# Folding a row stage (x + bias + two matrix products) into the tiles of a graph layer, with the layer's sum turned round

## The reference, cut to what matters

```python
xn = layernorm(x)
x = x + gnn(xn, edge_index, W1, b1, W2, b2) + mix(xn, W_qkv, b_qkv, W_out, b_out)
x = x + ffn(layernorm(x), ...)
# gnn: z = relu(agg(xn @ W1) + b1); z = relu(agg(z @ W2) + b2), agg over 200000 edges and self loops
# mix: attn = v + q2 @ kv / sqrt(N); return attn @ W_out + b_out
```

## Time and profile before

| | |
|---|---|
| median of 3 runs | 2124.17 us (2123.45 to 2128.42) |
| profiled execution, its own time | 2122.97 us |
| its span, first to last instruction | 2121.1 us |
| TensorE busy | 1900.7 us (90%) |
| VectorE, ScalarE, GpSimd busy | 1179.8, 878.9, 289.1 us |
| granted TensorE clock, mean | 0.951 of full speed |

### The profile page before, as it was taken

How to read it: one execution, slowest core, us unless ns; L and a number is a source line. 1 busy time by engine, 2 the same in 40 slices (tenths; PEclk the granted TensorE clock), 3 DMA queues, 4 the chain that set the end, 5 groups by cost and what they waited for, 6 DMA issues and landing times. The chain is left out here.

```text
span 2121.1 us, 37341 instructions
## 1 busy us (share of the span) xinstructions
PE 1900.7 (90%) x11735; PEld 1126.4 (53%) x11735; DVE 1179.8 (56%) x2764; ACT 878.9 (41%) x1997; POOL 289.1 (14%) x418
## 2 busy tenths in 40 slices
PE   3069997969999999999999799999999999999588
PEld 3045555845555555555555445555555555555477
DVE  6368872255666656566666235555555555555422
ACT  2157770035555555555555323333333333333200
POOL 3502222310000000000000200000000000000033
PEclk7579998989999999999999999999999999999789
DMA  3113325922222222222222344334343434342078
GB/s 92 31 43 112 111 98 180 285 81 107 107 91 121 91 121 91 116 96 102 110 91 121 120 152 141 141 134 148 127 154 123 156 123 156 125 146 102 20 235 249
DMA packets 106576, 262.52 MB, mean 124 GB/s; under 512 B 15682, under 2 KB 73386, under 8 KB 93978
## 3 DMA queue, kind: packets, MB, share of 16 engines
q1 hardware_dynamic: 76245, 225.23, 29.8%
q10 hardware_dynamic: 28116, 32.06, 4.3%
q0 software_dynamic: 2176, 4.75, 0.8%
HBM read 138.39 MB, written 124.42 MB: 124 GB/s over the span
## 5 line engine op out<-in xcount | busy, mean ns | idle before, releaser
L1344 PE MATMUL ps<-hs,at 128*128 128x512 f16 x2401 | 670.5, 378 | 3.3 <-POOL at L1261 3.3
L1539 PE MATMUL ps<-big,at 128*128 128x512 f16 x2401 | 559.7, 380 | 5.9 <-DMA at<-at_scratch 5.9
L1391 ACT CAST at<-ps 128x392 f16<-128x392 f32 x784 | 375.0, 486 | 430.3 <-PE ps L1333 408.4
L1333 PE MATMUL ps<-big 128*128 128x98 f16 x3136 | 465.0, 209 | 11.2 <-DVE big L1289 11.2
L1333 PEld LDWEIGHTS ps<-big 128*128 128x128 f16 x3136 | 298.4, 98 | 151.4 <-issue 10.8
L1539 PEld LDWEIGHTS ps<-big,at 128*128 128x128 f16 x2401 | 233.5, 98 | 255.6 <-issue 10.5
L1344 PEld LDWEIGHTS ps<-hs,at 128*128 128x128 f16 x2401 | 229.9, 97 | 146.3 <-POOL at L1261 3.5
L1289 DVE TENSOR_TENSOR big<-big,key_lo 128x1024 f16<-128x1024 f16 x392 | 268.5, 685 | 0.0
L1289 DVE TENSOR_TENSOR big<-big,key_hi 128x784 f16<-128x784 f16 x392 | 219.6, 560 | 17.5 <-POOL big L1251 7.6
L1751 POOL TENSOR_TENSOR key_lo<-key_lo,big 128x512 f32<-128x512 f32 (+1 forms) x49 | 61.8, 1262 | 708.0 <-ACT big L1713 708.0
L1300 DVE TENSOR_TENSOR big<-ps,big 128x256 f32<-128x256 f32 x49 | 20.8, 425 | 208.4 <-ACT big L1399 208.4
(11 more groups left out here) (275 smaller groups left out, 2218.4 us busy)
## 6 DMA issues: line engine op xcount, KB each, us to landing
at_scratch<-at SPq DMA_DIRECT2D x49, 1568.0 KB, 5.2
at<-at_scratch SPq DMA_DIRECT2D x49, 1568.0 KB, 6.5
xT_scratch<-big SPq DMA_DIRECT2D x98, 128.0 KB, 1.8
big<-xT_scratch SPq DMA_DIRECT2D x49, 256.0 KB, 3.5
wT_scratch<-big ACTq DMA_DIRECT2D x49, 256.0 KB, 2.1
hs<-wT_scratch SPq DMA_DIRECT2D x49, 256.0 KB, 3.4
big<-in_x_dram SPq DMA_DIRECT2D x96, 128.0 KB, 2.5
base_scratch<-big ACTq DMA_DIRECT2D x48, 128.0 KB, 4.1
```

The source lines that it names most:

```text
L1333: te.matmul(ps[:, BANKS[i // UW % len(BANKS)], i % UW * KC:(i % UW + 1) * KC], lhsT=hot_lo[:, s, :].rearrange("p (q k r) -> p q k r", k=P, ...
L1344: mm = te.matmul(ps[:, 2 + b, :], lhsT=at[:, b, k * P:(k + 1) * P], rhs=hs[:, k, :], start=(k == 0), stop=(k == T - 1))
L1391: a.copy(to.rearrange("p k (i j) -> p k i j", j=WIN), ps[:, BANKS[m % len(BANKS)], 0:UW * KC].rearrange("p (i k j) -> p k i j", i=UW, j=WI ...
L1539: mm = te.matmul(ps[:, b, :], lhsT=at[:, b, k * P:(k + 1) * P], rhs=hs2[:, k, :], start=(k == 0), stop=(k == T - 1))
```

## The change

Stage 0 and `base_scratch` go. Layer 2 loads x and the turned rows itself (128 and 256 KB a tile), GpSimd adds `bvo` to x there, TensorE makes the four products at step 3 of the 49 (`mix`), and VectorE adds them in `norm`. `wvo`, `mkv` and `bvo` get buffers of their own.

The layer 2 sum is turned round: `hs2` is now the stationary operand (four blocks of 128x128) and the block of `at` the moving one (128 columns), so each of 49 steps is four matmuls of 128 columns instead of one of 512. High and low halves add up in PSUM and the sum comes out turned already. So the copy of the low half, `gather`, and `turn` go; `multiply` moves from step 12 to 6.

In layer 1 only places move: `bias` from after batch 5 to 6, `multiply` from build step 28 to 36, `relu` from after unit 12 to 13.

```diff
-        stream(0, big_f, lambda t: xT_dram[...], x, [wvo[:, 0, :], wvo[:, 1, :], mkv[:, 0, :], mkv[:, 1, :]], bvo, base_dram)
...
-                        if i == 5 and reached(t, 1):
+                        if i == 6 and reached(t, 1):
                             bias(t - 1, 1 - b)
...
-                        if i == 28 and reached(t, 1):
+                        if i == 36 and reached(t, 1):
                             multiply(t - 1, 1 - b)
...
-                        if m == 12 and reached(t, 1):
+                        if m == 13 and reached(t, 1):
                             relu(t - 1, 1 - b)
...
-                    sp.dma_start(base_in[0:rows(t), b, :], base_dram[...]).then_inc(base_loaded[b], 16)
+                    sp.dma_start(base_in[0:rows(t), b, :], x[...]).then_inc(base_loaded[b], 16)
+                    sp.dma_start(turned_in[:, b]..., xT_dram[...]).then_inc(base_loaded[b], 16)
...
-                            pe.wait_ge(agg_ready, t - 1)
-                    mm = te.matmul(ps[:, b, :], lhsT=at[:, b, k * P:(k + 1) * P], rhs=hs2[:, k, :],
-                                   start=(k == 0), stop=(k == T - 1))
+                            pe.wait_ge(aggT_ready, t - 1)
+                    for h in range(2):
+                        for c in range(CB):
+                            mm = te.matmul(ps[:, b, c * NT:(c + 1) * NT], lhsT=hs2[:, k, h * C + c * P:h * C + (c + 1) * P],
+                                           rhs=at[:, b, k * P:(k + 1) * P], start=(k == 0 and h == 0 and c == 0),
+                                           stop=(k == T - 1 and h == 1), skip_group_check=True)
...
-                def turn(t, b):
...
+                def mix(t, b, u):
+
+                    pe.wait_ge(base_loaded[b], 32 * u + 32)
+                    if reached(t, 1):
+                        pe.wait_ge(x1_ready, t)
+                    for i, w in enumerate((wvo[:, 0, :], wvo[:, 1, :], mkv[:, 0, :], mkv[:, 1, :])):
+                        mm = te.matmul(ps[:, 2, 0:C], lhsT=turned_in[:, b, i, :], rhs=w, start=(i == 0), stop=(i == 2 * CB - 1))
+                    mm.then_inc(mixed, 1)
...
-                            for at_k, do in ((6, turn), (12, multiply), (31, turn_x), (37, logits)):
+                            if k == 3:
+                                mix(t - 1, *shifted_slot(b, u, -1, 2))
+                            for at_k, do in ((6, multiply), (31, turn_x), (37, logits)):
...
-                def gather(t, b):
-                    dve.wait_ge(low_ready, t + 1)
-                    v.tensor_tensor(agg[0:NT, b, :], ps[0:NT, b, 0:C], low[0:NT, b, :], ALU.add).then_inc(agg_ready, 1)
...
-                    dve.wait_ge(base_loaded[b], 16 * u + 16)
+                    dve.wait_ge(mixed, t + 1)
+                    dve.wait_ge(biased, t + 1)
+                    v.tensor_tensor(base_in[0:NT, b, :], ps[0:NT, 2, 0:C], base_in[0:NT, b, :], ALU.add).then_inc(zb_ready, 1)
...
-                    a.copy(low[0:NT, b, :], ps[0:NT, b, C:2 * C]).then_inc(low_ready, 1)
-                    act.wait_ge(agg_turned, t + 1)
-                    a.copy(aggT[:, b].rearrange("p a b -> p (a b)"), ps[:, 2, 0:CB * NT]).then_inc(aggT_ready, 1)
+                    if reached(t, 2):
+                        act.wait_ge(multiplied, t - 1)
+                    a.copy(aggT[:, b].rearrange("p a b -> p (a b)"), ps[:, b, 0:CB * NT]).then_inc(aggT_ready, 1)
...
+                    if within(t, T - 2):
+                        pool.wait_ge(base_loaded[b], 32 * u + 64)
+                        g.tensor_tensor(base_in[:, b, :], base_in[:, b, :], bvo, ALU.add).then_inc(biased, 1)
```

More of the change, by code:

```diff
@@ L85, in gps_layer @@
     at_dram = nc.dram_tensor("at_scratch", (T, P, T * P), F16, kind="Internal").ap()
-    base_dram = nc.dram_tensor("base_scratch", (N, C), F32, kind="Internal").ap()
     xT_dram = nc.dram_tensor("xT_scratch", (T, P, 2 * CB * NT), F32, kind="Internal").ap()
@@ L140, in gps_layer @@
         eps = sb("eps", [P, 1])
+        wvo = sb("wvo", [P, CB, C])[:, :, :]
+        mkv = sb("mkv", [P, CB, C])[:, :, :]
+        bvo = sb("bvo", [P, C])[:, :]
         ps = life.enter_context(nc.psum_tensor("ps", [P, 8, 512], F32))
@@ L157, in gps_layer @@
         bqk = take([P, 2 * C])
-        wvo = take([P, CB, C])
         bvw = take([P, C])
-        bvo = take([P, C])
-        mkv = take([P, CB, C])
         brow = take([3, 2 * C], BF16)
         ones3 = take([3, P], BF16)
-        AT_USED = 2 * CB * C + 2 * C + CB * C + 2 * C + CB * C + C + P // 2
+        AT_USED = 2 * CB * C + 2 * C + C + C + P // 2
         ones = sb("ones", [P, 2])
@@ L1056, in _ @@
                         act.wait_ge(s_out[b], 16 * (len(range(b, T, NB)) + past_in(b)))
-        stream(0, big_f, lambda t: xT_dram[bass.ds(t, 1)].rearrange("t p n -> (t p) n"), x,
-               [wvo[:, 0, :], wvo[:, 1, :], mkv[:, 0, :], mkv[:, 1, :]], bvo, base_dram)
         BATCH = 7
@@ L1481, in gps_layer @@
             take = carve(big_f[:, T * C:])
-            agg = take([P, 2, C])
-            low = take([P, 2, C])
             aggT = take([P, 2, CB, NT])
@@ L1486, in gps_layer @@
             base_in = take([P, 2, C])
+            turned_in = take([P, 2, 2 * CB, NT])
             x1 = take([P, 2, C])
@@ L1504, in gps_layer @@
             x1_out, w_out = [sem(f"x1_out{b}") for b in range(2)], [sem(f"w_out{b}") for b in range(2)]
-            summed, low_ready, agg_ready = sem("l2_summed"), sem("l2_low_ready"), sem("l2_agg_ready")
-            agg_turned, aggT_ready, multiplied = sem("l2_agg_turned"), sem("l2_aggT_ready"), sem("l2_multiplied")
+            summed, aggT_ready, multiplied = sem("l2_summed"), sem("l2_aggT_ready"), sem("l2_multiplied")
             x1_ready, ln_step, xn2_ready = sem("x1_ready"), sem("l2_ln_step"), sem("xn2_ready")
@@ L1512, in gps_layer @@
             acc_ready = sem("acc_ready")
+            biased, mixed = sem("l2_biased"), sem("l2_mixed")
             block = stage.enter_context(nc.Block())
@@ L1525, in tile @@
                         sp.wait_ge(x1_ready, t - 1)
-                    sp.dma_start(base_in[0:rows(t), b, :], base_dram[bass.ds(t * NT, rows(t)), :]).then_inc(base_loaded[b], 16)
+                    sp.dma_start(base_in[0:rows(t), b, :], x[bass.ds(t * NT, rows(t)), :]).then_inc(base_loaded[b], 16)
+                    sp.dma_start(turned_in[:, b].rearrange("p a b -> p (a b)"),
+                                 xT_dram[bass.ds(t, 1)].rearrange("t p n -> (t p) n")).then_inc(base_loaded[b], 16)
                 pipeline(sp, tile, T, 2)
@@ L1623, in norm @@
                                            in1=b2b[0:NT, :], op0=ALU.mult, op1=ALU.add).then_inc(zb_ready, 1)
-                    dve.wait_ge(zb_ready, t + 1)
-                    dve.wait_ge(base_loaded[b], 16 * u + 16)
+                    dve.wait_ge(mixed, t + 1)
+                    dve.wait_ge(biased, t + 1)
+                    v.tensor_tensor(base_in[0:NT, b, :], ps[0:NT, 2, 0:C], base_in[0:NT, b, :], ALU.add).then_inc(zb_ready, 1)
+                    dve.wait_ge(zb_ready, 2 * t + 2)
                     if reached(t, 2):
@@ L1680, in tile @@
                         divide(t, b)
-                    if within(t, T - 1):
-                        gather(t + 1, 1 - b)
-                    if reached(t, 0):
                         split(t, b)
                 dve.wait_ge(w2_loaded, 32)
-                pipeline(dve, tile, T, 2, lead=1)
+                pipeline(dve, tile, T, 2)
                 dve.wait_ge(s_added, T)
@@ L1748, in tile @@
                 def tile(t, b, u):
[L1750 to L1754, removed]
+                    if within(t, T - 2):
+                        pool.wait_ge(base_loaded[b], 32 * u + 64)
+                        g.tensor_tensor(base_in[:, b, :], base_in[:, b, :], bvo, ALU.add).then_inc(biased, 1)
+                    if reached(t, 0):
+                        pool.wait_ge(wt_ready, t + 1)
+                        g.tensor_tensor(w_acc[:, :, 0:rows(t)], w_acc[:, :, 0:rows(t)], wt[:, b, :, 0:rows(t)], ALU.add).then_inc(w_added, 1)
+                        pool.wait_ge(w_added, t + 1)
+                pipeline(pool, tile, T, 2, lead=2)
         with ExitStack() as stage:
@@ L1875, in _ @@
                 v.tensor_copy(pmat.rearrange("p a b -> p (a b)"), ps[:, 2:4, :].rearrange("p a b -> p (a b)"))
-        stream(1, final_rest, lambda t: wT_dram[bass.ds(t, 1)].rearrange("t p n -> (t p) n"), x1_dram,
+        stream(0, final_rest, lambda t: wT_dram[bass.ds(t, 1)].rearrange("t p n -> (t p) n"), x1_dram,
                [pmat[:, p, :] for p in range(HB)], bfb, out)
```

## The result

The changed kernel takes 2066.56 us (median; 2065.42 to 2069.17) against 2124.04 before: a ratio of 0.9727, 95% interval 0.971 to 0.9744, 57.5 us less. The forecast was 2062 us, its range 2050 to 2100. The profiled execution (2069.17 us, a span of 2066.8) is the slowest of the four, so its parts add up to 54.3 us less than the span of before.

What follows compares the result with a forecast made beforehand. The layers were taken as bound by TensorE's own instruction stream plus its stalls. Stage 0 -102.9, layer 1 -36.0 and layer 2 +77.5 made -61.4 us on 2122.97, 2061.6; the median 2062.8, taken as 2062 us, range 2050 to 2100.

Steps and rivals of the forecast that it cites:

- Stage 0, -102.9: Removing stage 0, from its first load at 332.50 to layer 1's first work at 435.44, gives its whole length, -102.9 us.
- The sign named for this: Start of layer 1: its iota was to come at 332 to 333 us if the forecast held.
- Layer 1, -36.0: Layer 1, multiply at step 36: its wait for keep's copy goes, 0.75 us a tile, 48 times, -36.0 us.
- The 28.2 us that the wait row names: Layer 1: TensorE idle time on multiply's wait for keep's copy, 48 times; taken as the gain's lower bound.
- Bias and relu: Layer 1: their later places cost nothing, bias hidden by a ring of four batches, relu with 0.5 us of cover.
- Layer 2's stream, 0.056 us a pair: Layer 2's sum: 9604 matmuls of 128 columns with loads, 0.056 us each, adding 0.37 us a tile.
- The slower rival: Layer 2's sum: loads space the 128-column stream; above 0.0624 us a pair slower than before, at 98 ns 2465 us; chance 0.11.
- The exposed f32 load: Layer 2, ahead of mix and multiply: f32 loads behind 128-column f16 matmuls cost 0 to 12.9 us, taken as 5.1.
- Turn and its wait, -0.60 us a tile: Layer 2: dropping turn saves 0.60 us a tile, of which 0.33 was a wait for VectorE's gather.
- VectorE's cover: Layer 2, between split's end at 19.2 and the next norm at 21.3: 2.1 us of cover, 1.7 before.
- The longer loop: Layer 2: rival that its loop of 952 instructions is fetched anew each pass, 40 to 46 us, 2102 to 2108; chance 0.06.
- The sum.: Whole kernel: -102.9 - 36.0 + 77.5 = -61.4 us on the execution's 2122.97, giving 2061.6.

Runs made afterwards that it cites:

- the tiny iota: The changed kernel with a two-column iota on GpSimd right behind its partition_all_reduce: 2061.8 us, ratio 0.97.

## Why the prediction was right, and where it was off

- **Stage 0, -102.9: off by 7.5 us, the largest miss.** Its mechanism held, the stage and all its transfers are gone. The step that failed is "layer 1's first instruction then stands where that load stood". Layer 1 begins with GpSimd's iotas, and GpSimd still had its change from the all-reduce ahead of it. The sign named for this, the iota at 332 to 333 us, failed: it came at 341.49. In the kernel before, the change lay inside stage 0. It can be read there: the pair of MODIFY_POOL_CONFIG stands at 332.6, the first bias addition starts at 341.36, though the loads were issued from 332.50 on the earlier trace rows and TensorE began on them at 335.48. VectorE's first addition had to wait for it. Layer 1's iota had such a pair too, at 435.3 to 435.4, and started at 435.44: that row showed it only where the change was already made. I saw a first tile that started late and took it for part of the stage, when it was a cost of the neighbour.

```profile
L1018 POOLq MODIFY_POOL_CONFIG  x2: 11/11/11, 332.6 to 332.6; - x2
...
341.36 0.71 POOL L1018 TENSOR_TENSOR big<-big,at 128x256 f32<-128x256 f32 x1 [16.07 <-issue]
```

- **Layer 1, -36.0: measured -37.3.** The loss was 0.78 us a tile and not 0.75, and the run with that edit alone gives it to multiply's place. The 28.2 us that the wait row names would have been 9 us too few: the distance of two starts was the right reading. Bias and relu cost nothing, as said; relu's two copies and the self loops stayed ahead of the first sum product.
- **Layer 2's stream, 0.056 us a pair: right.** 9604 pairs run at the distance that eight showed (0.0558 us over a row of 100), with TensorE busy for 16.92 of 16.92 us. The loads' own rows fill 15.59 us of it and space nothing. The slower rival needed 0.0624 us. The 81 ns of the Trainium skill ("TensorE: Matmul & The Clock Gate", section "Back-to-back issue gap") do not hold for this stream; the same section's 56 for isolated matmuls does, with loads.
- **The exposed f32 load, 5.1 us out of a range of 0 to 12.9: right in size.** 0.053 was taken, 0.056 measured, at two places a tile; the run with mix ahead of multiply removes one and gains 2.7 us.
- **Turn and its wait, -0.60 us a tile: right for the change as a whole, wrong as a reason for the turned sum.** With mix at step 3, turn no longer waits, and in the run with the 512-column sum it costs 0.22 us (1505.43 to 1505.65); so 0.38 of the 0.60 would have gone anyway. In the folded kernel the turned sum saves these 0.22 and costs 0.37 and two exposed loads (0.11): 0.26 us a tile to the bad. That is its 16.92 against the 16.66 of a period in which norm is in time. The mean loss is 0.18, since the 512-column sum has its late periods. The forecast summed the edits against the kernel before and did not ask what one is worth beside the others.
- **VectorE's cover: enough.** The forecast gave 2.1 us with the turned sum. VectorE idles 1.59 us ahead of norm in the period shown by the windows, and turn_x comes 6.50 us after `multiply` in every tile but the last. With the 512-column sum and gather it is not quite enough: norm is late by 0.18 us in 21 tiles.
- **The longer loop: not fetched anew.** Between 1200 and 1890 us, in which the loop of layer 2 makes some 20 passes, no block of queue q8 is read, as in the earlier trace rows. All the instruction traffic is one small packet:

```profile
q14 instruction: 1, 0.01, 0.0%
```

  So a loop of 952 matmuls and loads ran without being fetched anew. Of the two statements of the Trainium skill ("Runtime: NRT & Kernel Launch", section "Instruction fetch mechanics"), the 2048 instructions agree with this and the window of two blocks of 256 does not.
- **The sum.** -61.4 forecast, -57.5 by the medians, -54.3 by the profiled executions, in which the parts can be told apart. There 7.5 us are GpSimd's change, 1.3 and 1.2 come back from the two layers, and 2.1 lie in all the rest, 1.4 of them in the preparation. That the two layers erred the other way is luck, and so is that the medians lie nearer to the forecast than the profiled execution does.

## What to carry to other kernels

When a stage is removed, look for what was hidden at its edges: a slow first instruction inside it belongs to whatever comes next, and stays. Price a stall by the distance of starts and not by the idle time of the row, and price each edit of a bundle against the bundle without it, since an edit that cures a wait is worth only the rest of what it saves once another has cured it. A step at a fixed place in a hand-written order may be the cheapest thing to move: one number was worth 36 of the 57 us.

## What the runs showed of the hardware

- GpSimd took 6.7 to 7.6 us between a partition_all_reduce and its next addition or iota, and none ahead of a memset (which starts 0.25 us after the all-reduce does). The time starts with the MODIFY_POOL_CONFIG that stands ahead of that instruction (334.2 in the changed kernel, 324.8 with the tiny iota), so a tiny one issued early hides it. A second such pair, when the change is made, costs nothing (332.5, iota at 332.62).
- 128-column f16 matmuls, each with a load of its own, run at 0.056 us each for a whole layer at a granted clock of 1.00, though each load's row is 98 ns. Four of them take 0.223 us, one of 512 columns 0.216.
- An f32 group behind 128-column f16 matmuls loses 0.056 us once (0.92 in place of 0.86 for four instructions); behind 512-column ones it loses nothing (0.86).
- A TensorE loop of 952 matmuls and loads passed some 20 times between 1200 and 1890 us with no q8 block read.
